# A graph layer on one core: the sort's comparisons, scans and picks, and the edge dots, read their second tensor from PSUM

## The reference, cut to what matters

```python
h = maximum(layernorm(x), 0)                       # x: 6250 x 128
edge_h = concatenate([h[src], edge_attr_128], 1)   # 100000 edges
edge_m = einsum('ef,of->eo', edge_h, a)            # a: 128 x 256
edge_e = exp(-leaky_relu(edge_m @ a_2[0], 0.2))
rowsum = segment_sum(edge_e, src, 6250)            # 0 -> 1e-12
h_prime = segment_sum(edge_e[:, None] * edge_m, src, 6250)
return x + h_prime / rowsum[:, None]
```

## Time and profile before

| | |
|---|---|
| median of 3 runs | 1390.6 us (1382.74, 1390.6, 1390.81) |
| span of the profiled execution | 1389.8 us |
| VectorE busy | 886.8 us (64%), 4800 instructions |
| GpSimd busy | 903.8 us (65%), 813 instructions |
| TensorE matmul busy | 736.8 us (53%), 5708 instructions |
| ScalarE busy | 625.0 us (45%), 2404 instructions |

### The profile page before, as it was taken

The page is one execution under the profiler, slowest core; times in us unless marked ns, Lnnn a source line. Parts: engine busy times, 40 slices in busy tenths (PEclk is TensorE's granted clock), DMA queues, the critical chain, the costliest instruction groups (busy, mean ns, idle before and its releaser), DMA issues.

```text
span 1389.8 us, 27531 instructions
## 1 busy us (share of the span) xinstructions
PE 736.8 (53%) x5708; PEld 619.2 (45%) x5709; DVE 886.8 (64%) x4800; ACT 625.0 (45%) x2404; POOL 903.8 (65%) x813
## 2 busy tenths in 40 slices
PE   2742115210052141323778767777776777787677
PEld 1731014100042130322666656666665666666565
DVE  7777598737767783885766665566554656532337
ACT  2675200430112123033665665657564567564556
POOL 3037897778887887877777777777777756632000
PEclk9865557555566565565676765667756667787999
DMA  9265303432223234237646776746875624503623
GB/s 241 77 205 154 111 10 115 143 121 73 74 83 119 73 96 132 71 104 258 215 152 193 225 228 199 222 137 202 238 211 178 213 73 141 146 34 143 223 61 92
DMA packets 166199, 200.94 MB, mean 145 GB/s; under 512 B 18423, under 2 KB 125014, under 8 KB 165846
## 3 DMA queue, kind: packets, MB, share of 16 engines
q1 hardware_dynamic: 126612, 90.42, 22.6%
q10 hardware_dynamic: 14402, 56.44, 12.9%
q0 software_dynamic: 25088, 53.04, 10.9%
HBM read 140.12 MB, written 59.70 MB: 144 GB/s over the span
## 4 chain that ended last, share of the span: by engine, by line
PE 34%; POOL 32%; issue 19%; DVE 9%; DVEq 2%; DMA 2%; ACT 2%; POOLq 0%; ACTq 0%; SPq 0%
POOL ordered_rows L435 32%; PE psum L664 24%; PE psum L657 7%; DVE acc L934 2%; PE psum L641 1%; DVE chosen L893 1%; DMA acc<-in_x 1%; DVE junk L882 1%; PE psum L614 1%; DVE hots L953 1%; DVE back L750 1%; DVEq L276 1%; DVE feed L843 1%; DVE feed L988 0%; DVE acc L941 0%
## 5 line engine op out<-in xcount | busy, mean ns | idle before, releaser
L435 POOL DMA_INDIRECT ordered_rows<-feed,dest x784 | 893.0, 1139 | 355.9 <-issue 274.8
L664 PE MATMUL psum<-back,hots 128*128 x2128 | 401.6, 365 | 11.6 <-DVE hots L953 6.6
L664 PEld LDWEIGHTS psum<-back,hots 128*128 128x128 f32 x2128 | 368.7, 269 | 70.6 <-issue 70.6
L554 ACT ACTIVATE dist<-node_id,back 128x128 bf16 x532 | 169.9, 389 | 297.0 <-PE psum L664 265.7
L641 PE MATMUL psum<-score_parts,place_hot 128*128 128x50 bf16 x2352 | 101.9, 206 | 302.1 <-DVE place_hot L877 300.3
L934 DVE TENSOR_TENSOR acc<-acc,psum 128x387 f32 (+1 forms) x133 | 74.3, 559 | 261.8 <-PE psum L664 229.7
L498 ACT ACTIVATE feed<-feed (+1 forms) x784 | 239.1, 387 | 0.0
L641 PEld LDWEIGHTS psum<-score_parts,place_hot 128*128 128x128 bf16 x2352 | 95.4, 111 | 310.8 <-DVE place_hot L877 307.2
L490 ACT ACTIVATE feed<-leaky (+2 forms) x98 | 20.4, 208 | 409.4 <-DVE leaky L906 409.4
L657 PE MATMUL psum<-zeros 1*128 1x387 bf16 x399 | 115.1, 407 | 166.7 <-issue 126.4
L882 DVE SCALAR_TENSOR_TENSOR junk<-feed,edge_w 128x128 f32<-128x128 f32 x784 | 174.3, 286 | 0.0
(11 more groups left out here) (141 smaller groups left out, 429.9 us busy)
## 6 DMA issues: line engine op xcount, KB each, us to landing
back<-ordered_rows ACTq DMA_DIRECT2D x98, 528.0 KB
feed<-in_edge_attr SPq DMA_DIRECT2D x97, 512.0 KB, 4.6
place_rows<-places SPq DMA_DIRECT2D x98, 256.0 KB
ordered_rows<-feed,dest POOLq DMA_INDIRECT x784
self_part<-acc ACTq DMA_DIRECT2D x1, 3234.0 KB, 11.3
feed<-self_part SPq DMA_DIRECT2D x1, 3234.0 KB
out<-feed SPq DMA_DIRECT2D x6, 448.0 KB
src_row<-in_src SPq DMA_DIRECT2D x1, 390.5 KB, 3.6
```

Of the source, the lines that this page charges most:

```text
L435: pool.indirect_dma_start(out=ordered, out_offset=bass.IndirectOffsetOnAxis(ap=dest[:, n:n + 1], axis=0), in_=feed[:, n * ROW:(n + 1) * RO ...
L554: act.activation(dist[:, u, :], node_id[:, bass.ds(wins[u], P)], ACT.Abs, scale=-1.0, bias=back[:, bass.ds(slots[u] + SRC, 1)]).then_inc(d ...
L664: last = pe.matmul(psum[:, bass.ds(outs[u], FEAT + 1)], hots[:, hot_buffer(k) * GT + u, :], back[:, bass.ds(slots[u], FEAT + 1)], start=Fa ...
```

## The change

For chunks 1 to 4 one tensor operand of each long VectorE instruction of the sort comes from PSUM. Bank 7 holds constants: edge_w, the bucket numbers in fp32, and a zero. ScalarE writes them once, behind the projection of the nodes (constants). The comparison reads the bucket numbers there; the scan reads the zero, broadcast, as its second tensor instead of hot; the dots of all groups read edge_w there. For the picks ScalarE copies each bucket's counts to one of six banks (0 to 5, in turn), and the pick reads the copy as in0 (copy_counts); each pick waits for its copy, each copy for the pick five before the one whose bank it takes. Chunk 0's sort stays as it was, but for where its small sums stand.

The sums of ranks of chunks 1 to 4 move to bank SCORES, from which the look-up writes and the picking reads. So the look-up of the first group behind a sort part is moved: it ran before that part, and now TensorE does it behind it, and behind a rank after the table is written. VectorE's nodes() waits for the three constants instead of the weights.

```diff
+            def constants():
+                act.wait_ge(table_done, 1)
+                act.copy(bank(CONSTS, EDGE_W, FEAT), edge_w[:, :]).then_inc(consts_done, 1)
+                act.copy(bank(CONSTS, NUMBERS, BUCKETS), bucket_no[:, :]).then_inc(consts_done, 1)
+                act.copy(bank(CONSTS, ZERO, 1), score_parts[:, 0, 0:1]).then_inc(consts_done, 1)
+
+            def copy_counts(c):
+                tiles = CHUNKS[c] * RT
+                act.wait_ge(ends_done, c + 1)
+                for b in range(BUCKETS):
+                    n = (c - 1) * BUCKETS + b
+                    if n >= COPIES:
+                        act.wait_ge(picks_done, n + BUCKETS - COPIES + 1)
+                    act.copy(bank(n % COPIES, COPY_AT, tiles), count[:, b * tiles:(b + 1) * tiles])\
+                       .then_inc(count_copied, 1)
...
                 if what == "stats":
                     nodes()
+                    constants()
+                elif what == "rank" and at[0] > 0:
+                    copy_counts(at[0])
...
+            def feeds(g0, n, before_sort):
+                if not before_sort:
+                    run_feeds(pe, g0, n, feed_group)
+                elif n > 1:
+                    run_feeds(pe, g0, n - 1, feed_group)
...
-            for what, *at in PLAN:
+            sorting = ("count", "rank")
+            for i, (what, *at) in enumerate(PLAN):
+                if what in ("feed", "pairs") and PLAN[i - 1][0] in sorting:
+                    if PLAN[i - 1][0] == "rank":
+                        pe.wait_ge(table_done, PLAN[i - 1][1] + 1)
+                    look_up(at[0] if what == "feed" else at[3])
...
+                numbers, none = bucket_no_bf[:, :], hot[:, 0:flat]
+                if c > 0:
+                    numbers, none = bank(CONSTS, NUMBERS, BUCKETS), bank(CONSTS, ZERO, 1).to_broadcast([P, flat])
...
-                                  bucket_no_bf[:, :].rearrange("p (b a) -> p b a", a=1).to_broadcast(shape),
+                                  numbers.rearrange("p (b a) -> p b a", a=1).to_broadcast(shape),
...
-                done(dve.tensor_tensor_scan(count[:, 0:flat], hot[:, 0:flat], hot[:, 0:flat], 0.0, ALU.add, ALU.max))
+                done(dve.tensor_tensor_scan(count[:, 0:flat], hot[:, 0:flat], none, 0.0, ALU.add, ALU.max))
...
-                    dve.scalar_tensor_tensor(out=picked[:, k * tiles:(k + 1) * tiles], in0=count[:, at],
+                    if c == 0:
+                        own_count = count[:, at]
+                    else:
+                        dve.wait_ge(count_copied, n - BUCKETS + 1)
+                        own_count = bank((n - BUCKETS) % COPIES, COPY_AT, tiles)
+                    dve.scalar_tensor_tensor(out=picked[:, k * tiles:(k + 1) * tiles], in0=own_count,
                                              scalar=shift[:, b:b + 1], in1=hot[:, at],
...
-                dve.wait_ge(weights_copied, 5)
+                dve.wait_ge(consts_done, 3)
                 start_group(0)
...
-                                             scalar=1.0, in1=edge_w[:, :], op0=ALU.mult, op1=ALU.mult,
+                                             scalar=1.0, in1=bank(CONSTS, EDGE_W, FEAT), op0=ALU.mult, op1=ALU.mult,
```

More of the change, by code:

```diff
@@ L223, in gnn_kernel, with ranks @@
         psum_sets = psum[:, 0:6 * 512].rearrange("p (s b f) -> p s b f", s=2, b=3)
-        SCORES, RANKS = 6, 7
+        SCORES = 6
+        SUMS, SHIFTS, TOTALS = 0, GT * BUCKETS, (GT + 1) * BUCKETS
+        CONSTS, EDGE_W, NUMBERS, ZERO = 7, 0, FEAT, FEAT + BUCKETS
+        assert SUMS + MAXT + RT <= SHIFTS and TOTALS < 512
+        def ranks(c, lo, n, rows=P):
+            return bank(7 if c == 0 else SCORES, lo, n, rows)
+        COPIES, COPY_AT = 6, 264
+        assert COPY_AT >= P + FEAT + 1 and COPY_AT + MAXT <= 512
         def bank(b, lo, n, rows=P):
@@ L233, in gnn_kernel @@
             centredT_done centredT_copied self_done self_copied self_saved parts_done acc_zero
-            edge_dots place_hot_done window_copied selected zed_done node_scores leaky_done prob_done tagged act_hot dve_hot dist_done
+            edge_dots consts_done count_copied place_hot_done window_copied selected zed_done node_scores leaky_done prob_done tagged act_hot dve_hot dist_done
             step_done acc_done inv_done scaled_done scaledT_done scaledT_copied out_ready self_added result_done
@@ L240, in gnn_kernel @@
          centredT_done, centredT_copied, self_done, self_copied, self_saved, parts_done, acc_zero,
-         edge_dots, place_hot_done, window_copied, selected, zed_done, node_scores, leaky_done, prob_done, tagged, act_hot, dve_hot, dist_done,
+         edge_dots, consts_done, count_copied, place_hot_done, window_copied, selected, zed_done, node_scores, leaky_done, prob_done, tagged, act_hot, dve_hot, dist_done,
          step_done, acc_done, inv_done, scaled_done, scaledT_done, scaledT_copied, out_ready, self_added, result_done,
@@ L603, in rank_sums @@
                 pe.wait_ge(ends_done, c + 1)
-                pe.matmul(bank(RANKS, 0, BUCKETS), below[:, :], ends[:, 1:BUCKETS + 1], start=True, stop=False)
-                pe.matmul(bank(RANKS, 0, BUCKETS), above[:, :], ends[:, 0:BUCKETS], start=False, stop=True)
-                pe.matmul(bank(RANKS, 64, 1, BUCKETS), ends[:, 0:BUCKETS], ones_bf[:, 0:1], start=True, stop=True)\
+                pe.matmul(ranks(c, SHIFTS, BUCKETS), below[:, :], ends[:, 1:BUCKETS + 1], start=True, stop=False)
+                pe.matmul(ranks(c, SHIFTS, BUCKETS), above[:, :], ends[:, 0:BUCKETS], start=False, stop=True)
+                pe.matmul(ranks(c, TOTALS, 1, BUCKETS), ends[:, 0:BUCKETS], ones_bf[:, 0:1], start=True, stop=True)\
                   .then_inc(shift_done, 1)
@@ L613, in pick_sums @@
                     pe.wait_ge(picks_done, c * BUCKETS + i * BB + k + 1)
-                    pe.matmul(bank(RANKS, P, tiles), ident[:, :], picked[:, k * tiles:(k + 1) * tiles],
+                    pe.matmul(ranks(c, SUMS, tiles), ident[:, :], picked[:, k * tiles:(k + 1) * tiles],
                               start=first and k == 0, stop=k == BB - 1, skip_group_check=True)\
@@ L621, in table_sums @@
                 pe.wait_ge(started_done, c + 1)
-                pe.matmul(bank(RANKS, P, npairs, 65), ones_bf[0:BUCKETS, 0:65], started[:, 0:npairs],
+                pe.matmul(ranks(c, SUMS, npairs, 65), ones_bf[0:BUCKETS, 0:65], started[:, 0:npairs],
                           start=True, stop=True).then_inc(pairs_done, 1)
@@ L693, in _ @@
                 elif what == "feed":
-                    run_feeds(pe, *at, feed_group)
+                    feeds(*at, PLAN[i + 1][0] in sorting)
                 elif what == "pairs":
@@ L758, in rank_chunk @@
                 dve.wait_ge(shift_done, c + 1)
-                done(dve.tensor_scalar(shift[:, :], bank(RANKS, 0, BUCKETS), -1.0, None, ALU.add))
+                done(dve.tensor_scalar(shift[:, :], ranks(c, SHIFTS, BUCKETS), -1.0, None, ALU.add))
                 for b in range(BUCKETS):
@@ L772, in rank_chunk @@
                 ri, pa, pb, pc = (v[:, 0:tiles] for v in (rank_i, part_a, part_b, part_c))
-                done(dve.tensor_copy(ri, bank(RANKS, P, tiles)))
+                done(dve.tensor_copy(ri, ranks(c, SUMS, tiles)))
                 low, mid = (P - 1).bit_length(), (GT - 1).bit_length()
@@ L788, in rank_chunk @@
                 fp = first_pair
-                done(dve.tensor_copy(first_pair_i[:, :], bank(RANKS, 64, 1, BUCKETS)))
+                done(dve.tensor_copy(first_pair_i[:, :], ranks(c, TOTALS, 1, BUCKETS)))
                 done(dve.tensor_scalar(first_pair_i[:, :], first_pair_i[:, :], low, None, ALU.arith_shift_right))
@@ L797, in rank_chunk @@
                 win, tile, wrap = (v[:, 0:npairs] for v in (row_win, row_tile, row_wrap))
-                done(dve.tensor_scalar(win, bank(RANKS, P, npairs, 65), -1.0, None, ALU.add))
+                done(dve.tensor_scalar(win, ranks(c, SUMS, npairs, 65), -1.0, None, ALU.add))
                 done(dve.tensor_tensor(tile, pair_no[0:65, 0:npairs], win, ALU.subtract))
```

## The result

| | before | after |
|---|---|---|
| median of 4 runs each | 1386.7 us (1378.8 to 1390.8) | 1299.6 us (1294.5 to 1305.7) |
| after / before | | 0.937, 95% interval 0.933 to 0.941 |
| span of the profiled execution | 1389.8 us | 1304.0 us |
| memset of acc (end of the feeding stage) | 639.4 us | 556.8 us |
| from it to the end | 750.5 us | 747.2 us |

The forecast was 1314, with a range of 1296 to 1352. The gain lies where it was put: 82.6 of the 85.8 us between the two spans come before the memset. Lines have moved with the edit: L445 is the scatter (before L435), L340 SP's hand-over (L330), L930 place_hot (L877), L935 the dots (L882), L946 the picking (L893), L792 the comparison (L744), L798 the scan (L750), L821 the picks (L768), L673 the look-up (L641), L826 the cast that takes the picks' sum (L773), L994 the memset (L941). L490 is new, the copies of the counts.

A forecast was written before the change was run, and what follows sets the result against it. GpSimd's scatters, held by VectorE's sorts, bound the feeding stage; TensorE the pairs. Waits gave 99.2 - 3.3 - 6 - 4 - 6 = 80, stretches 76; 77 taken: 1389.8 - 77 = 1312.8, plus 0.8, say 1314 us, range 1296 to 1352.

The forecast's parts named there:

- The scatters are let through: Sorts: a long VectorE instruction with one tensor in PSUM leaves a scatter at 0.96 us; 130 of 140 us return.
- Rival C: Sorts: one long read from SBUF is enough to block, so GpSimd's stalls stay; 1394 us, chance 0.07.
- E: Feeding stage: GpSimd stays the bound because VectorE sheds waits of its own; memset at 506, 1257 us, chance 0.04.
- What it brings is VectorE's wait, not GpSimd's stall: Feeding stage: VectorE becomes the bound and can save at most its 99.2 us of wait, less what the edit adds.
- PSUM costs nothing: VectorE's dots, picks, comparison and scan: an operand in PSUM leaves durations unchanged, dots at 286 ns.
- Rival D: Chunks 1 to 4: comparison and scan stream at half pace from PSUM, 106 us more; 1420 us, chance 0.05.
- A: Dots and picks: an operand in PSUM has a fixed price of 57 ns; 1336 to 1350 us, chance 0.12.
- ScalarE's copies: Picks of chunks 1 to 4: copies keep up; the extra semaphore wait costs 1 us a sort, 4 in all.
- Rival B: Picks: the hand-over between ScalarE and VectorE sets their pace, 60 us at 0.3 each; about 1370 us, chance 0.08.
- Look-up and start: Five look-ups behind sort parts cost VectorE 6 us; waiting for the constants moves GpSimd's start by 3.3 us.
- Sort 1 runs GpSimd dry: Chunk 1's sort: GpSimd idles about 12 us where it was held for 38; 6 us of VectorE's wait remain.
- From there VectorE is the bound: From 304 us to the memset: VectorE's own work sets the pace, putting the memset at 563 us.

The follow-up runs named there:

- e7: Changed kernel with the scan of chunks 1 to 4 reading hot in SBUF twice again: 1329.9 us, ratio 0.963 to the kernel before.
- e8: Changed kernel without ScalarE's copies, the picks reading the counts in SBUF: 1306.4 us, ratio 0.949 to the kernel before.
- e2: Changed kernel with the comparison reading bucket numbers in SBUF again, on the chip where the kernel before took 1892.5 us: 1887.7 us, ratio 1.000.
- e10: Kernel before with one edit, a zero in PSUM as the scan's second tensor in chunks 1 to 4: 1330.5 us, ratio 0.969.
- e9: Changed kernel with the dots reading edge_w in SBUF again: 1305.9 us, ratio 0.951 to the kernel before.
- e5: Changed kernel run again with no edit: 1297.7 us against 1385.5 for the kernel before on the same chip, ratio 0.937.
- e3: Changed kernel with the picks reading counts in SBUF, no copies, on the chip where the kernel before took 1892.5 us: 1888.1 us.

## Why the prediction was right

*The scatters are let through.* Right, and by the mechanism named. 136.2 us of scatters went (130 assumed). Undone for the scan (e7), the picks (e8) and the comparison (e2), each brings back its own stalls and no other's; done for the scan alone (e10), it frees the scans and no other. Rival C (blocking stays) fell with the first sort's rows, and so did E (GpSimd stays the bound), which had the memset at 506 us. The Trainium skill (SBUF — State Buffer, section "Who interferes with whom") says that an instruction of VectorE with at most one input in SBUF, outside its two-port modes, doesn't contend with GpSimd: this trace agrees, with 1.25 us for the longest scatter. The same section of the Trainium skill says that an instruction with two inputs in SBUF contends with a GpSimd instruction that reads SBUF, but infers that tensor_tensor doesn't hold the descriptor generation of a DMA that GpSimd issues: for the indirect ones of this kernel the trace shows 12.29 us beside one, so here the measurement decides.

*What it brings is VectorE's wait, not GpSimd's stall.* This was the step that made the size right. The stalls were 140 us and the wait 99.2; the gain is 82.6 us up to the memset. Redone with what was measured, the prediction's sum from the waits, 99.2 - 3.3 - 6 - 4 - 6 = 80, reads 99.2 - 2.2 (later start of sort 1) - 5.5 (look-ups) - 1.3 (picks) - 8.0 (left after sort 1) = 82.2. e7 shows the rule at work: 67 us of stalls back, 20 us of wait back, 20 us of time. e8: 26 us of stalls back, nothing. The same stalls cost more the more of them there are: removing the scan's 64 us first (e10) brought 65.6, adding them last (e7) costs 20. Until GpSimd has something to spare, the wait and the stall are the same.

*PSUM costs nothing.* Right: dots 281 against 286 ns, small comparison 5983 against 5989, large comparison 11812 and scan 23486 ns against 11.82 and 23.49 us. Rival D (half pace) is out, and A with e9.

*ScalarE's copies.* Right in size, with the parts a little off. A copy of 224 columns takes 347 ns, they start 0.31 us apart where VectorE lets them, and the picks' pitch went from 0.370 to 0.376 us (chunk 1) and from 0.363 to 0.384 (chunk 2), and not at all in chunks 3 and 4: 1.3 us in all, where 4 was taken. Even this may not be the copies: e8 has none, and its pitches are 0.380, 0.363, 0.268 and 0.265 us. A copy waits for the pick six before it, the last to read its bank, and not five as the part on the change has it. Rival B (hand-over) is out.

*Look-up and start.* Forecast 6 and 3.3 us. The start came 3.1 us later. The five pickings behind the sort parts wait 1.27 to 1.61 us, where they waited 0.05 to 0.29: 5.5 us more. Part of both is made up where VectorE would have waited anyway: sort 1 started only 2.2 us later (168.34 against 166.11).

*Sort 1 runs GpSimd dry.* Right to about a microsecond: group 14 scattered at 246.8 (248 forecast), idle for 1.7 + 11.1 us (12), sort 1 started at 168.3 (169.4). The wait left behind it was forecast as 6 us at start_group(26): that one is 5.7, but start_group(25) waits 2.3 as well, so 8.0 were left.

*From there VectorE is the bound.* Right. The memset came at 556.8 and not 563, and this is the whole difference to the forecast: 2 us stood already at the start of chunk 2's sort (302.0 against 304), and the group's pitch was 4.50 us where 4.65 was taken, 3 us over 21 groups. The 4.65 came from the earlier trace rows, a stretch of the kernel before in which place_hot took 0.54 us and a group 4.6 to 4.95. Of the 0.15 us the dots make 0.04 (e9's pitch is 4.54). The rest comes and goes with place_hot, which is 0.71 us at times in e8 and 0.49 in after; why was not looked for.

*GpSimd to spare.* 20 us forecast. From start_group(30) on it is 14.4 us ahead of what VectorE needs, 22 at 35, 25 at 42 and 35 at 47. e8 is the test: 26 us of stalls in it moved nothing, though the lead was down to 4.4 us at start_group(42). GpSimd ran dry for 4.8 us in sort 3 and 3.6 in sort 4, where 10 to 15 was taken.

*The pairs stage unchanged.* 750.5 before, 747.2 and 736.9 in two profiles of the changed kernel. The bounds of 10 us were too narrow, and the second profile shows the prediction's own last sign of being wrong, a change of over 10 us behind the memset, though no instruction there was touched. Over the kernels of the usual chips it is 736.5 to 754.2, and the granted clock goes with it (0.76 to 0.74). The medians of the changed kernel (1299.6 and 1297.7) lie 14 to 16 below the forecast: about 6 are the memset, the rest is this stage and its noise. That this noise fell on the side of a larger gain is luck, not reasoning.

## What to carry to other kernels

Where GpSimd issues indirect DMAs beside long VectorE instructions, look for single issues as long as a VectorE instruction; if that instruction reads two tensors in SBUF, one of them in PSUM (a broadcast zero will do for a scan) frees the issue at no cost in VectorE's time. Take the gain from the wait that comes back to the bounding engine and not from the sum of the stalls, and fix the longest instruction first: here one operand of the scan brought 66 of 83 us up to the memset, and 200 copies for the picks brought nothing. A gain of this kind is bound to who is the bound: on a chip where VectorE was late by itself the same stalls cost nothing that could be measured.

## What was not expected of the hardware

A run of short instructions holds a scatter as one long one does: picks of 0.44 us each, 0.36 us apart, held one for 15.3 us (e8), while a scatter beside eight dots of 0.29 us, 0.21 apart, takes 1.03, and none outside the sorts of the kernel before took over 1.2. Two spans of one kernel, the memset at the same place, differed by 10 us in the pairs stage alone (e5), with the mean granted clock of that stage at 0.75 and 0.76. And one chip ran all kernels 1.4 times slower, with VectorE's dots 1 to 3 us apart in some groups and waits of up to 20.8 us in front of the picking (e3), while single instructions of VectorE and GpSimd had their usual durations (the scan 23.49 us, a scatter 0.96) and TensorE's granted clock was lower (0.62 over the span against 0.68 to 0.70): most of the loss is between instructions, and its cause was not found.
